# Attention stage: the bias of q and k enters as a matmul, features are made by one relu and one exponential in two buffers, and the state is summed in SBUF

## The reference, cut to what matters

```
qkv = x @ Wqkv.T + bqkv
q = (elu(q) + 1 + 1e-4) / sqrt(16);  k = elu(k) + 1 + 1e-4
kv_cumsum = cumsum over tokens of k (outer) v;  k_cumsum = cumsum over tokens of k
out = (q . kv_cumsum) / (q . k_cumsum + 1e-4)
out = out @ Wout.T + bout;  layer norm of it times gamma plus beta
```

## Time and profile before

| | us |
|---|---|
| median of 3 runs | 2542.86 (2541.41 to 2543.53) |
| the profiled execution, its own time | 2543.91 |
| its span, first to last instruction | 2542.0 |
| PE, DVE, POOL, ACT busy | 2341.0, 2127.0, 2032.2, 1937.6 |

### The profile page before, as it was taken

How to read it: one execution, slowest core, us unless ns; L and a number is a source line. 1 busy time by engine, 2 the same in 40 slices (tenths; PEclk the granted TensorE clock), 3 DMA queues, 4 the chain that set the end, 5 groups by cost and what they waited for, 6 DMA issues and landing times. The chain is left out here.

```text
span 2542.0 us, 75165 instructions
## 1 busy us (share of the span) xinstructions
PE 2341.0 (92%) x22402; PEld 1676.2 (66%) x22402; DVE 2127.0 (84%) x5242; ACT 1937.6 (76%) x4422; POOL 2032.2 (80%) x3359
## 2 busy tenths in 40 slices
PE   1599999999995699999999999999699999999998
PEld 1266666666663588888888888888356666565665
DVE  6599999999996477777777777777699999999997
ACT  2688888888882677777777777777688888888885
POOL 0599999999993477877877877877598989989896
PEclk9799999999998799999999999999899999999999
DMA  1355555555554122222222222222155555555555
GB/s 36 79 113 118 112 113 116 114 113 116 113 97 77 33 56 54 54 56 54 54 57 54 54 56 54 54 55 55 36 109 110 115 109 116 110 115 110 112 113 116
DMA packets 730847, 215.31 MB, mean 85 GB/s; under 512 B 662182, under 2 KB 730534, under 8 KB 730790
## 3 DMA queue, kind: packets, MB, share of 16 engines
q1 hardware_dynamic: 730790, 214.65, 41.3%
HBM read 20.51 MB, written 16.78 MB: 15 GB/s over the span
## 5 line engine op out<-in xcount | busy, mean ns | idle before, releaser
L577 PE MATMUL ffn_ps_gu<-wgu_hi,ffn_xT 128*128 128x512 f16 (+1 forms) x3072 | 737.1, 363 | 50.0 <-DMA ffn_xT<-ffn_x_hl 50.0
L577 PEld LDWEIGHTS ffn_ps_gu<-wgu_hi,ffn_xT 128*128 128x128 f16 x3072 | 300.7, 98 | 334.9 <-DMA ffn_xT<-ffn_x_hl 52.1
L577 PE MATMUL ffn_ps_gu<-wgu_lo,ffn_xT 128*128 128x512 f16 (+1 forms) x1536 | 430.5, 362 | 0.0
L531 ACT ACTIVATE ffn_quarter<-ffn_y,offsets 128x960 int16<-128x960 f32 (+2 forms) x264 | 282.7, 1071 | 185.5 <-DVE ffn_y L467 184.9
L587 PE MATMUL ffn_ps_down<-wd_hi,ffn_hT 128*128 128x256 f16 x2816 | 350.6, 273 | 23.1 <-DVE x_sb L456 14.7
L887 ACT ACTIVATE attn_expo<-attn_ps_qk,attn_neg_bqk,attn_unscale 128x128 f32<-128x128 f32 x512 | 192.8, 456 | 230.1 <-POOL attn_q_rows L834 225.1
L512 POOL TENSOR_TENSOR ffn_h_hl<-ffn_q,ffn_h_scale_hi 128x704 f16<-128x704 f16 x256 | 351.4, 1373 | 15.9 <-DVE ffn_h_scale_lo L473 13.2
L513 POOL TENSOR_TENSOR ffn_h_hl<-ffn_q,ffn_h_scale_lo 128x704 f16<-128x704 f16 x256 | 354.1, 1383 | 0.0
L587 PEld LDWEIGHTS ffn_ps_down<-wd_hi,ffn_hT 128*128 128x128 f16 x2816 | 264.7, 98 | 106.2 <-issue 36.7
L436 DVE TENSOR_REDUCE ffn_per_block<-ffn_hx 128x60 f32<-128x960 f32 (+2 forms) x264 | 298.5, 1131 | 42.4 <-ACT ffn_hx L561 20.0
L467 DVE TENSOR_TENSOR ffn_y<-ffn_hx,ffn_per_block 128x960 f32<-128x960 f32 (+2 forms) x264 | 294.7, 1116 | 0.0
(11 more groups left out here) (197 smaller groups left out, 5840.4 us busy)
## 6 DMA issues: line engine op xcount, KB each, us to landing
attn_v_eo<-attn_v_nat SPq DMA_DIRECT2D x512, 34.0 KB, 1.9
x_sb<-in_L_attn_x SPq DMA_DIRECT2D x128, 128.0 KB, 2.3
out<-x_sb SPq DMA_DIRECT2D x128, 128.0 KB, 2.1
ffn_xT<-ffn_x_hl SPq DMA_TRANSPOSE x256, 2.4
ffn_hT<-ffn_h_hl SPq DMA_TRANSPOSE x256, 3.6
attn_xT<-attn_x_hl SPq DMA_TRANSPOSE x128, 2.4
attn_oT<-attn_o_hl SPq DMA_TRANSPOSE x128, 2.4
raw_qkvo<-in_L_attn_Wqkv SPq DMA_DIRECT2D x1, 768.0 KB, 5.3
```

The lines of the kernel that those rows point to most:

```text
L531: nc.scalar.activation(quarter[:, back], y[:, back], ACT.Identity, bias=offsets[:, 0:1], scale=4.0 / HALF_MIN).then_inc(S["quarter"], 1)
L577: last = nc.tensor.matmul(ps_gu[par][:, a:b], xT[par][:, c, :], w[:, k, a:b], start=(n == 0), stop=(n == len(terms) - 1))
```

## The change

Features. `expo` becomes two buffers, `u_one` goes. A bf16 matmul of 3 rows by 128 columns opens each of the four columns of `ps_qk` and brings the bias plus 1, scaled to the units of `ps_qk` and split into three bf16 parts (`bqk3`, against `ones3`). ACT then makes relu(1 - scale x ps_qk) for all 512 columns in one instruction, then the exponential; DVE takes the maximum with scale x ps_qk straight from PSUM. q_rows moves from POOL to ACT.

State. `ps_kv` becomes two banks, one for each half of 64 tokens, written afresh for each tile. The halves are row tiles of PE (rows 0 to 63 and 64 to 127) and stand together right behind v. DVE masks each into SBUF (`first`, `second`), POOL adds `before` and `first` into `mid`, DVE adds `mid` and `second` into the next `before`. L976 goes.

Besides, k transposes and v share one bank, and orders change: on PE num follows the state and the scores follow num; on POOL the norm's small operations and L839 move forward; on ACT the split of o (L896) moves behind the norm of i+3. `pipeline` loses its argument `every`. The set-up builds `bqk3` from a row-wise copy of the biases on 3 partitions.

```diff
-        u_one = sb("u_one", [P, 2 * DC, P])
-        expo = sb("expo", [P, 2 * DC, P])
+        expo = pair("expo", [P, 2 * DC, P])
-        ps_kT = psum("ps_kT", [P, 512])
+        ps_kT_v = psum("ps_kT_v", [P, 512])
-        ps_v = psum("ps_v", [P, 512])
-        ps_kv = psum("ps_kv", [P, HEADS, VW])
+        ps_kv = psum("ps_kv", [P, 2, 512])
...
 # DVE, behind L783
+                if valid(i, N):
+                    ready(dve, "kv_done", i)
+                    freed(dve, "mid", i, 1)
+                    nc.vector.tensor_tensor(first[:], half_state(0), own_head(), ALU.mult).then_inc(S["kv_first"], 1)
+                if valid(i, N) and not (isinstance(i, int) and i == N - 1):
+                    nc.vector.scalar_tensor_tensor(second[:], half_state(1), column(keep, i + 1), own_head(), ALU.mult, ALU.mult).then_inc(S["kv_second"], 1)
+                if valid(tf, N):
+                    ready(dve, "exp", tf)
+                    nc.vector.scalar_tensor_tensor(expo[oth][:], ps_qk[:], unscale[:, 0:1], expo[oth][:], ALU.mult, ALU.max).then_inc(S["feat"], 1)
...
 # DVE, behind L792
-                if valid(i, N):
-                    ready(dve, "kv_mid", i)
-                    nc.vector.tensor_tensor(mid[par][:], ps_kv[:], own_head(), ALU.mult).then_inc(S["mid"], 1)
-                if valid(tf, N):
-                    ready(dve, "exp", tf)
-                    nc.vector.tensor_tensor(expo[:], u_one[:], expo[:], ALU.max).then_inc(S["feat"], 1)
-                    ready(dve, "kv_end", i)
-                    nc.vector.scalar_tensor_tensor(before[oth][:], ps_kv[:], column(keep, i + 1), own_head(), ALU.mult, ALU.mult).then_inc(S["before"], 1)
+                    ready(dve, "mid", i)
+                    ready(dve, "kv_second", i)
+                    freed(dve, "num_done", i + 1, 2)
+                    nc.vector.scalar_tensor_tensor(before[oth][:], mid[par][:], column(keep, i + 1), second[:], ALU.mult, ALU.add).then_inc(S["before"], 1)
...
 # POOL
-                    for j in range(2):
-                        last = nc.gpsimd.tensor_scalar(q_rows[par][:, :, j, :], expo[:, 0:DC, :], FEAT_EPS, of_pair[:, j:j + 1], ALU.add, ALU.mult)
-                    last.then_inc(S["q_rows"], 1)
...
+                if valid(i, N):
+                    ready(pool, "kv_first", i)
+                    if not (isinstance(i, int) and i == 0):
+                        pool.wait_ge(S["before"], i)
+                    freed(pool, "num_done", i, 2)
+                    nc.gpsimd.tensor_tensor(mid[par][:], before[par][:], first[:], ALU.add).then_inc(S["mid"], 1)
...
 # ACT
+                    for j in range(2):
+                        last = nc.scalar.activation(q_rows[par][:, :, j, :], expo[par][:, 0:DC, :], ACT.Identity, bias=of_pair_eps[:, j:j + 1], scale=of_pair[:, j:j + 1])
+                    last.then_inc(S["q_rows"], 1)
                 if valid(tf, N):
                     ready(act, "qk_done", tf)
-                    freed(act, "q_feat", tf, 1)
-                    freed(act, "q_rows", tf, 1)
-                    freed(act, "kT_done", tf, 1)
-                    for c in range(2 * DC):
-                        last = nc.scalar.activation(expo[:, c, :], ps_qk[:, c, :], ACT.Relu, bias=neg_bqk[:, c:c + 1], scale=unscale[:, 1:2])
-                    last.then_inc(S["relu"], 1)
-                    for c in range(2 * DC):
-                        nc.scalar.activation(u_one[:, c, :], ps_qk[:, c, :], ACT.Identity, bias=one_bqk[:, c:c + 1], scale=unscale[:, 0:1])
+                    freed(act, "q_rows", tf, 2)
+                    freed(act, "k_odd", tf, 2)
+                    freed(act, "kT_done", tf, 2)
+                    nc.scalar.activation(expo[oth][:], ps_qk[:], ACT.Relu, bias=one[:], scale=unscale[:, 1:2]).then_inc(S["relu"], 1)
                     ready(act, "relu", tf)
...
 # PE
                     for col in range(2 * DC):
+                        at = slice(col * P, (col + 1) * P)
+                        nc.tensor.matmul(ps_qk[:, col, :], bqk3[:, at], ones3[:], start=True, stop=False)
                         for n, (aT, w) in enumerate(terms):
-                            last = nc.tensor.matmul(ps_qk[:, col, :], w[:, col * P:(col + 1) * P], aT, start=(n == 0), stop=(n == len(terms) - 1))
+                            last = nc.tensor.matmul(ps_qk[:, col, :], w[:, at], aT, start=False, stop=(n == len(terms) - 1))
...
+                    ready(pe, "k_nat", i)
+                    ready(pe, "v_nat", i)
+                    freed(pe, "kv_first", i, 1)
+                    if not (isinstance(i, int) and i == 0):
+                        pe.wait_ge(S["kv_second"], i)
+                    for c in range(DC):
+                        for s in range(2):
+                            own = v_nat[par][half(s), :, c * PAIRS:(c + 1) * PAIRS, :].rearrange("p a j w -> p j a w")
+                            last = nc.tensor.matmul(half_state(s)[:, c * 2 * PAIRS:(c + 1) * 2 * PAIRS, :].rearrange("p (j a) w -> p j a w", a=2),
+                                                    k_nat[half(s), c * P:(c + 1) * P], own, start=True, stop=True)
+                    last.then_inc(S["kv_done"], 1)
...
 # set-up, DVE
-            nc.vector.tensor_scalar(neg_bqk[:], bqk[:], -1.0, None, ALU.mult).then_inc(done, 1)
-            nc.vector.tensor_scalar(one_bqk[:], bqk[:], 1.0, None, ALU.add).then_inc(done, 1)
...
+            def three_parts(dst, v, n):
+                rest, part = spare3[:, 0, 0:n], part3[:, 0:2, 0:n]
+                for k in range(2):
+                    then(nc.vector.tensor_copy(part[:, k], v))
+                    then(nc.vector.tensor_tensor(v, v, part[:, k], ALU.subtract))
+                then(nc.vector.tensor_scalar(rest, part[:, 0], ident[0:3, 0:1], None, ALU.mult))
+                then(nc.vector.scalar_tensor_tensor(rest, part[:, 1], ident[0:3, 1:2], rest, ALU.mult, ALU.add))
+                then(nc.vector.scalar_tensor_tensor(dst, v, ident[0:3, 2:3], rest, ALU.mult, ALU.add))
...
+            then(nc.vector.reciprocal(qk_up[:], unscale[:, 0:1]))
+            then(nc.vector.tensor_scalar(spare3[:, 1, :], bqk_rows[:], 1.0, qk_up[0:3], ALU.add, ALU.mult))
+            three_parts(bqk3[:], spare3[:, 1, :], 2 * D)
```

More of the change, by code:

```diff
@@ L82, with pipeline @@
 ATTN_TURN = 4
-def pipeline(eng, step, n, ahead, behind, turn=TURN, every=2):
+def pipeline(eng, step, n, ahead, behind, turn=TURN):
     first, end = behind, n - ahead
@@ L593 @@
 ATTN_SEMS = ("sums", "stats", "var", "rstd", "shift", "xn", "x_hi", "x_split", "turn", "xT_even", "xT_odd", "qk_done", "relu", "exp", "feat", "k_even", "k_odd",
-             "q_feat", "q_rows", "v_done", "v_nat", "v_eo_even", "v_eo_odd", "kT_done", "k_nat", "scores_done", "masked", "kv_mid", "kv_end",
+             "q_feat", "q_rows", "v_done", "v_nat", "v_eo_even", "v_eo_odd", "kT_done", "k_nat", "scores_done", "masked", "kv_done", "kv_first", "kv_second",
              "mid", "before", "num_done", "den", "rden", "o_ready", "o_hi", "o_split", "oT_even", "oT_odd", "proj_done",
@@ L623, in attention @@
         o_scale = sb("o_scale", [P, 2])
-        bqk = sb("bqk", [P, 2 * DC])
-        neg_bqk = sb("neg_bqk", [P, 2 * DC])
-        one_bqk = sb("one_bqk", [P, 2 * DC])
+        bqk3 = sb("bqk3", [3, 2 * D], BF16)
+        one = sb("one", [P, 1])
         v_bias = sb("v_bias", [P, D])
@@ L633, in attention @@
         of_pair = sb("of_pair", [P, 2])
+        of_pair_eps = sb("of_pair_eps", [P, 2])
         z_eps = sb("z_eps", [P, 1])
@@ L638, in attention @@
         keep = sb("keep", [P, N])
[L640 to L641 removed]
+        prepare_attention(nc, sem, sbuf, N, CH, wqkv, bqkv, wout, bout, gamma, beta, ident, ident16, wqkv_hi, wqkv_lo, unscale, wout_hi, wout_lo, o_scale, bqk3, one,
+                          v_bias, rows, causal, diag, even, odd, of_pair, of_pair_eps, z_eps, ones3, bout3, feat_eps, keep)
         AHEAD, BEHIND = 4, 4
@@ L660, in attention @@
         scores = sb("scores", [P, 2, DC, 2, 2, SUB])
+        first, second = sb("first", [P, HEADS, VW]), sb("second", [P, HEADS, VW])
         mid = pair("mid", [P, HEADS, VW])
@@ L913, in _, with step @@
         def _(pe):
-            def step(i, m):
-                par, oth = m % 2, 1 - m % 2
+            def step(i, par):
+                oth = 1 - par
                 tf, tn, to = i + 1, i - 1, i - 2
[L918 to L924, removed]
                 if valid(i, N):
                     ready(pe, "feat", i)
-                    freed(pe, "k_nat", i, 1)
+                    ready(pe, "v_nat", i)
                     for c in range(DC):
-                        last = nc.tensor.transpose(ps_kT[:, c * P:(c + 1) * P], expo[:, DC + c, :], ident[:])
+                        last = nc.tensor.transpose(ps_kT[:, c * P:(c + 1) * P], expo[par][:, DC + c, :], ident[:])
                     last.then_inc(S["kT_done"], 1)
@@ L1001, in _, with prepare_attention @@
             pe.wait_ge(set_up, SET_UP)
```

(9 more changed lines are left out.)

81 lines of the change are left out of this document (40 added, 41 removed).

## The result

The changed kernel takes 2570.15 us (median of 4 runs, 2569.69 to 2570.93) against 2543.02 (2541.41 to 2543.53). The ratio is 1.0108 (95% interval 1.0091 to 1.0126, which leaves 1 out): slower by 27 us, where 2571 was forecast. The profiled execution has 2570.93 and a span of 2569.2.

The account below looks back on a forecast made before the run. The ACT-POOL ring over `expo` bounds the kernel at 7.343 us per tile; after the change PE bounds at 7.53. 2543.91 + 23.7 + 3.8 = 2571.4, said as 2571 us, range 2530 to 2605.

Parts of the forecast that it names:

- The ring: In attention, ACT and POOL wait for each other over the single `expo` buffer; claimed to set 7.343 us per tile.
- PE needs 6.85: PE's mean need per attention tile in the kernel before: 6.85 us of 7.343, 0.49 from being the bound.
- A bias term: Each 3-row matmul ahead of a `ps_qk` column costs PE 0.258 us, changes of shape included; four cost +1.03.
- State and scores: PE's two state halves and the scores, with the change to z: 1.74 us per tile instead of 1.93.
- PE's sum 7.53: PE's work per attention tile in the changed kernel, without waits: 7.53 us against 7.343, +23.7 us in all.
- The other engines stay below PE: Work per attention tile after the change: ACT 4.4 us, POOL 5.5, DVE 6.1, all covered by PE.
- Operations no row showed: New attention operations, estimated from similar rows: relu 0.68 us, q_rows on ACT 0.50, POOL's add 0.77, DVE's third operation 0.56.
- Set-up and first tile: Ahead of and at the start of attention: DVE's added bias work +5.2, SP -0.5, first tile -1; together +3.8 us.
- Rival A: The small bias matmuls on PE cost only their columns: -75 us, 2469; chance 10%.
- Rival D: Slower still: PE waits 0.2 a tile, with a new chain through `first` and `mid`, or the clock drops: 2595 to 2630; 12%.

Follow-up runs that it names:

- e5: The kernel before with two buffers for `expo` and nothing else: 2496.99 us, ratio 0.9819 to the kernel before.
- e9: e5 with DVE's copy of mid moved ahead of the divide's last operation: 2477.23 us, ratio 0.9728 to the kernel before.
- e3: The changed kernel without the four bias matmuls of q and k: 2435.4 us, ratio 0.9571 to the kernel before.
- e1: The changed kernel with both operands of the q,k bias matmuls filled with zeros to 128 rows: 2463.93 us, ratio 0.9685 to the kernel before.
- e4: The kernel before with four 3-row bias matmuls of zeros added and nothing else of the change: 2633.92 us, ratio 1.0353 to the kernel before.
- e8: The changed kernel with q,k and z bias operands zero-filled to 128 rows and the scores ahead of num: 2458.76 us, ratio 0.967 to the kernel before.

## Why the prediction was right, step by step

- *The ring sets 7.343.* Right: e5 removes it alone and the period falls to 6.966. No wait of the relu for POOL is left in the profile after.
- *PE needs 6.85 in the kernel before.* Too low, for a reason that cancels in part: the tile I read it from, the one in four with L976, doesn't have the wait for mid that the other three have (+0.17 in the mean, e5 against e9), and it began behind a wait, with a weight load that wasn't hidden (-0.055). It is 6.97, and 6.80 with mid copied in time (e5, e9). The forecast of the changed kernel doesn't rest on it, for the change takes that wait away; only the 0.055 went into 7.53, and there it met the terms (0.02) and the state and scores (0.03), which were taken too low. That 7.53 is so close is in part luck.
- *A bias term costs 0.258, four 1.03.* Measured 0.263 and 1.053 (e3), of which 0.227 are columns and 0.826 changes of shape (e1).
- *State and scores 1.74 instead of 1.93.* After: 0.67 + 1.10 = 1.77.
- *PE's sum 7.53, nothing else in its way.* Measured 7.506; PE has no wait in the profile after. From the kernel before with the terms (e4, 8.025) to the changed one it is 0.52, and the parts give 0.50: L976 0.17, state and scores 0.16, the wait for mid 0.17.
- *The other engines stay below PE.* Right: by their busy time between 900 and 1740 us ACT needs 4.6 a tile, POOL 5.5 and DVE 5.9, where 4.4, 5.5 and 6.1 were forecast.
- *Operations no row showed.* The relu of 512 columns took 0.78 (0.68 taken, bounds 0.50 to 0.83), a q_rows on ACT 0.59 (0.50), mid on POOL 0.76 (0.77), before from SBUF 0.49 (0.56). All lay beside PE, so the errors cost nothing. The rows:

```profile
L892 ACT ACTIVATE attn_q_rows<-attn_expo,attn_of_pair_eps,attn_of_pair 128x256 f32<-128x256 f32 x256 | 138.0, 587 | 0.0
L900 ACT ACTIVATE attn_expo<-attn_ps_qk,attn_one,attn_unscale 128x512 f32<-128x512 f32 x128 | 99.5, 777 | 76.0 <-PE attn_ps_qk L943 76.0
L861 POOL TENSOR_TENSOR attn_mid<-attn_before,attn_first 128x272 f32<-128x272 f32 x128 | 97.7, 763 | 82.7 <-DVE attn_first L792 82.7
```

- *Set-up and first tile +3.8.* The set-up came out at +5.25: DVE's added work was sized right (5.3), but the 0.5 that SP's issue was to give back came to less than 0.1. The first tile came out at -0.5 instead of -1, and the end of attention at +1.5, which the forecast had not. So that 2571 is nearly exact is luck: periods 3 us too long in all stand against 2.7 us that were left out.
- *Rival A* (small matmuls are free but for their columns) names the kernel that should have been built: it is e1 in effect, 2464, where 2469 was given. It failed for the kernel as written because of the shape, not of the matmul. *Rival D*'s chain through first and mid exists (POOL's wait in the last row above), but it reaches PE in no run: what reaches PE in e8 is another chain, from num through the divide and the split to the transpose of x.

The Trainium skill's page TensorEngine Tiling (Array Packing), section Tiling Modes, Key Properties, says that a change of tiling mode drains the engine. The time agrees in every run here: 0.09 to 0.10 us at each change of the rows or columns used, nothing where only the streamed columns change; the drain itself no trace shows. The price in the Trainium skill's TensorE: Matmul & The Clock Gate, section Back-to-back issue gap, 134 cycles for 128 columns, fits e1's terms, 0.057 us each, once they have the rows of their neighbours. The same section calls this the gap of a single matmul and gives about 81 ns for a stream of weight loads and matmuls; e1's rows, a load to each matmul, are 56 ns apart, and the measurement decides.

## What to carry to other kernels

Before adding a small matmul, read off the trace what the distance of two starts becomes where the shape changes, and multiply by the changes a tile, not by the matmuls. If it is the bound, pad the small operand with zeros to its neighbours' rows, or put the small ones together; and order blocks of one shape beside each other, after a look at who waits for the block that comes later by it (e8). A PE busy share of 100% does not say that PE waits for nothing: compare the distances of starts between a tile that waited and one that didn't, and take the sum of an engine from more than one turn of the loop.

## What the runs showed that I had not expected

A matmul with 125 rows of zeros is 0.21 us cheaper than one without them (e1, per term). The first weight load behind a wait costs 0.05 us more, which no busy column shows. L872, the subtraction that was L861, takes 0.67 us where it took 0.87, and L841, a neighbour on POOL, 0.61 in the mean where L840 of the same form takes 0.48:

```profile
L872 POOL TENSOR_TENSOR attn_o_hl<-attn_o,attn_o_hl 128x256 f16<-128x256 f32 x128 | 85.9, 671 | 120.4 <-ACT attn_o_hl L914 120.4
...
L841 POOL TENSOR_SCALAR attn_k_eo<-attn_expo,attn_odd 128x256 f32<-128x256 f32 x128 | 77.7, 607 | 12.0
```

In both cases it goes with what DVE does at the time. In the kernel before, L861 starts 0.35 ahead of the end of DVE's maximum of two SBUF tensors (L801) and takes 0.87; in e5 it overlaps L801 by 0.65 in 23 of 93 tiles and takes 1.19 there. In e9, which differs from e5 only in the order on DVE, it starts when L801 is done and takes 0.67. L841 overlaps DVE's addition to x (L769) in every tile between 950 and 1600 us, and one of the two is longer each time: in 44 tiles L841 takes 0.75 and L769 0.46, in 43 tiles 0.48 and 0.65. What decides between them was not tried.
